# One run of state sums a batch, a scan over the states, and blocks laid out by GpSimd in a linear-attention layer

## The reference

```
xn  = layernorm(x)
q, k, v = split(xn @ wqkv);  q = relu(q); k = relu(k)        # 16 heads of 16 channels
num = q_t . sum_{s<=t} k_s v_s^T;  den = q_t . sum_{s<=t} k_s + 1e-5
attn = (num / den) @ wo
cw  = top-2 router weights of sigmoid(xn @ Wr), normalised   # 8 experts
routed = sum_{e<4} cw_e * (silu(xn Wg_e) * (xn Wu_e)) Wd_e
         + (cw_4 + cw_6) * xn + cw_7 * relu(xn)
conv = causal depthwise convolution of xn, 4 taps, + conv_b
out = x + attn + routed + conv
```

## Time and profile before

| | us |
|---|---|
| median of 3 runs | 1347.9 (1345.97 to 1350.45) |
| the profiled execution, its own time | 1346.54 |
| its span, first to last instruction | 1344.8 |
| PE busy | 1313.8 (98%) |
| DVE busy | 1114.9 (83%) |
| POOL busy | 814.9 (61%) |
| ACT busy | 738.3 (55%) |

### The profile page before, as it was taken

How to read it: one execution, slowest core, us unless ns; L and a number is a source line. 1 busy time by engine, 2 the same in 40 slices (tenths; PEclk the granted TensorE clock), 3 DMA queues, 4 the chain that set the end, 5 groups by cost and what they waited for, 6 DMA issues and landing times.

```text
span 1344.8 us, 54748 instructions
## 1 busy us (share of the span) xinstructions
PE 1313.8 (98%) x24384; PEld 1136.4 (85%) x24384; DVE 1114.9 (83%) x2566; ACT 738.3 (55%) x1545; POOL 814.9 (61%) x679
## 2 busy tenths in 40 slices
PE   4899999999999999999999999999999999999997
PEld 3788888888888888888888888888888888888886
DVE  4888888888888888988888988888888889888885
ACT  4555665555664565654555655555645656545561
POOL 2755666755666656657556666556566566575554
PEclk9999999999999999999999999999999999999999
DMA  4011111111111211111111111121111111111110
GB/s 148 34 66 65 51 48 34 65 65 66 46 53 34 65 65 64 35 45 55 66 65 51 48 35 65 65 65 42 56 35 66 65 65 35 34 65 50 50 49 18
DMA packets 46779, 73.73 MB, mean 55 GB/s; under 512 B 6480, under 2 KB 42192, under 8 KB 42448
## 3 DMA queue, kind: packets, MB, share of 16 engines
q1 hardware_dynamic: 46544, 70.24, 15.1%
HBM read 53.18 MB, written 17.04 MB: 52 GB/s over the span
## 4 chain that ended last, share of the span: by engine, by line
PE 97%; DVE 1%; SPq 1%; ACT 1%; DMA 1%; issue 0%; DVEq 0%
PE ring L300 51%; PE scores L300 17%; PE ring L408 7%; PE ring L422 6%; PE scores L357 5%; PE state_sum L371 4%; PE ring L440 2%; PE scores L310 2%; PE scores L339 2%; DMA x_t<-in_L_attn_x_dram 1%; SPq L257 0%; DVE cT L775 0%; ACT qp L517 0%; DVE sm L753 0%; ACT xn L528 0%
## 5 line engine op out<-in xcount | busy, mean ns | idle before, releaser
L626 POOL TENSOR_TENSOR hid<-hid,cwb 128x512 f32<-128x512 f32 x128 | 169.8, 1327 | 202.6 <-DVE hid L783 200.8
L775 DVE SCALAR_TENSOR_TENSOR cT<-xT,conv_ws,cT 128x512 f32<-128x512 f32 x192 | 288.8, 1543 | 0.0
L614 POOL TENSOR_TENSOR x_t<-x_t,same 128x1024 f32<-128x1024 f32 x32 | 77.1, 2409 | 264.3 <-ACT same L524 264.3
L540 ACT ACTIVATE sg<-ring 128x512 f32<-128x512 f32 x128 | 76.7, 599 | 281.5 <-PE ring L300 281.5
L300 PE MATMUL ring<-xl,wgu_h 128*128 128x512 f32 x512 | 212.0, 414 | 0.0
L300 PE MATMUL ring<-xh,wgu_l 128*128 128x512 f32 x512 | 202.5, 396 | 0.0
L300 PE MATMUL ring<-xh,wgu_h 128*128 128x512 f32 x512 | 201.8, 394 | 0.0
L630 POOL TENSOR_TENSOR hl<-hid,hh 128x512 fp32r<-128x512 f32 x128 | 193.2, 1509 | 0.0
L783 DVE TENSOR_TENSOR hid<-ring,sg 128x512 f32<-128x512 f32 x128 | 88.2, 689 | 110.9 <-PE ring L300 110.9
L480 ACT ACTIVATE yh<-yT 128x256 fp32r<-128x256 f32 x128 | 53.5, 418 | 228.9 <-DVE yT L796 228.9
L753 DVE TENSOR_TENSOR sm<-scores,causal_s 128x512 f32<-128x512 f32 x256 | 158.7, 681 | 20.4 <-PE scores L357 20.2
(11 more groups left out here) (110 smaller groups left out, 3542.6 us busy)
## 6 DMA issues: line engine op xcount, KB each, us to landing
cwb<-cw_rows SPq DMA_DIRECT2D x32, 1024.0 KB, 4.6
x_t<-in_L_attn_x_dram SPq DMA_DIRECT2D x32, 512.0 KB, 4.4
out_dram<-x_t SPq DMA_DIRECT2D x32, 512.0 KB, 2.9
cw_rows<-cwt SPq DMA_DIRECT2D x128, 2.0 KB, 1.4
sm<-in_L_attn_wqkv_dram SPq DMA_DIRECT2D x2, 384.0 KB, 5.5
sm<-in_L_ffn_Wg_dram SPq DMA_DIRECT2D x2, 256.0 KB, 4.2
sm<-in_L_ffn_Wu_dram SPq DMA_DIRECT2D x2, 256.0 KB, 5.8
cwb<-in_L_ffn_Wd_dram SPq DMA_DIRECT2D x1, 512.0 KB, 4.2
```

The lines of the kernel that those rows point to most:

```text
L614: pool.tensor_tensor(xb, xb, same[:, :, :], ALU.add).then_inc(s_base1, 1)
L626: pool.tensor_tensor(hid[:, e, :], hid[:, e, :], cwb[:, e, :], ALU.mult).then_inc(s_hid, 1)
L775: ins = dve.scalar_tensor_tensor(out=cT[:, c, :], in0=xT[:, j % 2, c, n:n + BT], scalar=conv_ws[:, c, n:n + 1], in1=cT[:, c, :], op0=ALU.m ...
```

## The change

The bank of `state_sum` is gone, and with it the running sum on PE. `state_sums` forms the sums of all eight chunks of a batch in one run, after `output(0)` (chunk halves h in the score banks 2 and 3, each chunk in its own columns). ACT copies them to `sums`, laid out with nine places for each state element: place 0 is the state carried in, 1 to 8 the chunks. DVE adds them up in one `tensor_tensor_scan` over 64 x 9 elements, where `keep` is 0 at place 0 and 1 elsewhere; the result, `states`, lies in the memory of `qks_tok`. Place 8 is copied to place 0 of `sums` for the next batch (at a sequence's end a zero is written). POOL multiplies `states` with the mask of equal heads into `state_bd`, which now has a slot for each chunk, in two instructions of 1024 elements a partition; it reads `states` with the chunk as the outer index, so that neighbouring elements of the read lie nine floats apart. The scores of the next batch wait for ACT's copies, as they use the same banks.

The freed bank makes the ring four banks wide. Gates go two tiles ahead of the numerators, which are made for two tiles at once (`numerators(0)`, `numerators(1)`), and DVE, ACT and POOL get lists in that order. The cross products wait once a group for all blocks (`s_bd`).

```diff
-state_bd = sb("state_bd", [P, 4, D])
+sums = sb("sums", [P, C * BLK, NCH + 1])
+state_bd = sb("state_bd", [P, NCH, D])
+keep = sb("keep", [P, C * BLK, NCH + 1])
...
+states = qks_tok[:, :, :].rearrange("p g n -> p (g n)")[:, 0:C * BLK * (NCH + 1)].rearrange(
+    "p (c n) -> p c n", c=C * BLK)
...
-SB = [bank(f"scores{f}") for f in range(ROWS)]
-ring = ctx.enter_context(nc.psum_tensor("ring", [P, 3, BT], F32))
-R = [ring[:, 0, :], ring[:, 2, :]]
-MID = ring[:, 1, :]
-ST_ = bank("state_sum")
-ST = ST_[:, 0:C * BLK].rearrange("p (g n) -> p g n", g=C)
-GB = [R[0], R[1]]
-UB = [R[1], R[0]]
-NB2 = [(R[0], MID), (MID, R[1])]
+low = ctx.enter_context(nc.psum_tensor("scores", [P, ROWS, BT], F32))
+SB = [low[:, f, :] for f in range(ROWS)]
+SUMS = low[:, 2:4, 0:T * C * BLK].rearrange("p h (t c) -> p h t c", t=T)
+ring = ctx.enter_context(nc.psum_tensor("ring", [P, 4, BT], F32))
+B = [ring[:, b, :] for b in range(4)]
+GB = [B[0], B[1], B[2], B[1]]
+UB = [B[2], B[3], B[3], B[0]]
+NUM = [ring[:, 0:2, :], ring[:, 1:3, :]]
...
-VB = [SB[2], SB[3], R[0], R[1]]
-OB = [MID, R[0], R[1], MID]
+VB = [SB[2], SB[3], B[3], B[0]]
+OB = [B[0], B[2], B[1], B[3]]
...
         if u:
             pe.wait_ge(s_sm, at(s, j, U * ROWS, ROWS))
         else:
-            pe.wait_ge(s_qp2, at(s, j, C, k * C + C))
             pe.wait_ge(s_ktok, at(s, j, C, k * C + C))
+            pe.wait_ge(s_sums, at(s, j, 2, 2 * k + 2))
...
-    def state_sum(s, j, k, n):
...
+    def state_sums(s, j, k):
+        pe.wait_ge(s_qp2, at(s, j, C, k * C + C))
+        pe.wait_ge(s_ktok, at(s, j, C, k * C + C))
+        for t in range(T):
+            for g in range(C):
+                for m in range(PPG):
+                    rows = slice(BLK * m, BLK * m + BLK)
+                    for h in range(2):
+                        toks = slice(h * HALF, (h + 1) * HALF)
+                        ins = mm(SUMS[rows, h, t, g * BLK:(g + 1) * BLK], ktok[toks, t, g, rows],
+                                 vp[toks, t, g * PPG + m, 0:3:2, :], start=t == 0 and g == 0, stop=True,
+                                 skip_group_check=True)
         ins.then_inc(s_st, 1)
...
+                if t < 2:
+                    pe.wait_ge(s_out, at(s, j, T, 2 * t + u + 1))
+                elif t == 2:
+                    pe.wait_ge(s_gu, at(s, j, T, 1 + u))
...
+                    pe.wait_ge(s_y, at(s, j, T, 2))
+                product((GB, UB)[u][t], [(wgu_h[:, u, t, c, :], wgu_l[:, u, t, c, :], xh[:, p, c, :],
+                                         xl[:, p, c, :]) for c in range(C)]
...
-        def numerators(t):
...
-                state_sum(s, j, 0, 2 * t + 1)
...
-                n = 2 * t + h
-                pe.wait_ge(s_bd, chunk_at(s, j, n))
+        def numerators(v):
+            pe.wait_ge(s_sg, at(s, j, T, 2 * v + 2))
+            pe.wait_ge(s_sm, at(s, j, U * ROWS, ROWS * (v + 1)))
+            for tt in range(2):
+                t = 2 * v + tt
...
+                    gs = slice((tt * C + g) * HALF, (tt * C + g + 1) * HALF)
+                    for par in range(2):
+                        for m in range(PPG):
+                            pair = g * PPG + m
+                            for h in range(2):
+                                toks = slice(h * HALF, (h + 1) * HALF)
+                                window = vp[toks, t, pair, par:par + 2, :].rearrange("p a d -> p (a d)")
+                                mm(NUM[v][BLK * m:BLK * m + BLK, h, gs], window,
+                                   sm[toks, v, tt, 2 * pair + par, :], start=tt == 0 and par == 0 and g == 0,
+                                   stop=False, skip_group_check=True)
+            pe.wait_ge(s_bd, at(s, j, 1, 1))
+            for tt in range(2):
+                for h in range(2):
+                    n = 2 * (2 * v + tt) + h
+                    if j == 0 and n == 0:
+                        continue
+                    for g in range(C):
+                        gs = slice((tt * C + g) * HALF, (tt * C + g + 1) * HALF)
+                        for w in range(2):
+                            rows = slice(w * HALF, (w + 1) * HALF)
+                            cols = slice(g * P + w * HALF, g * P + (w + 1) * HALF)
+                            ins = mm(NUM[v][rows, h, gs], state_bd[:, n, cols],
+                                     qT[:, g, n * HALF:(n + 1) * HALF], start=False, stop=True,
+                                     skip_group_check=True)
             ins.then_inc(s_num, 1)
-            if t < T - 1:
-                state_sum(s, j, 0, 2 * t + 2)
...
-                scores(s, j, 0, 1)
-            if t == 1 and not last:
-                for c in range(C):
-                    turn_xn(s, j, 1, c)
+        gate_up(0)
+        scores(s, j, 0, 1)
+        gate_up(1)
+        numerators(0)
+        if not last:
+            for c in range(C):
+                turn_xn(s, j, 1, c)
+        gate_up(2)
+        gate_up(3)
+        numerators(1)
         if not last:
             heads(s, j, 1)
         for t in range(T):
-            if t == T - 1 and not last:
+            output(t)
+            if t == 0 and not last:
+                state_sums(s, j, 1)
+            if t == 2 and not last:
                 scores(s, j, 1, 0)
-                state_sum(s, j, 1, 0)
-            output(t)
...
         ins.then_inc(s_relu7, 1)
+        act.wait_ge(s_st, at(s, j, 1, k + 1))
+        for h in range(2):
+            copy(sums[:, :, 1 + h:NCH + 1:2].rearrange("p c t -> p t c"), SUMS[:, h, :, :]).then_inc(s_sums, 1)
         act.wait_ge(s_den, at(s, j, 1, k + 1))
         act.activation(dene[:, :, :], den[:, :, :], ACT.Copy, bias=EPS_DEN).then_inc(s_dene, 1)
...
         silu(0)
         first_tap()
-        high_y(0)
         silu(1)
         high_hid(0)
+        high_y(0)
         high_y(1)
         if not last:
             fill_xT(s, j, 1)
+        high_hid(1)
         silu(2)
         if not last:
             high_x(s, j, 1)
-        high_hid(1)
-        high_y(2)
         silu(3)
         high_hid(2)
+        high_hid(3)
+        high_y(2)
         high_y(3)
-        high_hid(3)
         if not last:
             heads(s, j, 1)
...
+    def blocks(s, j, k):
+        pool.wait_ge(s_scan, at(s, j, 1, k + 1))
+        for g in range(C):
+            ins = pool.tensor_tensor(state_bd[:, :, g * P:(g + 1) * P].rearrange("p n (m c) -> p n m c", m=PPG),
+                                     states[:, g * BLK:(g + 1) * BLK, 0:NCH].rearrange("p c n -> p n c")
+                                     .unsqueeze(2).to_broadcast([P, NCH, PPG, BLK]),
+                                     same_head_s[:, :].rearrange("p (m c) -> p m c", m=PPG).unsqueeze(1)
+                                     .to_broadcast([P, NCH, PPG, BLK]), ALU.mult)
+        ins.then_inc(s_bd, 1)
...
         if not last:
             normalise(s, j, 1)
         weigh(0)
-        low_y(0)
         weigh(1)
         low_hid(0)
+        low_y(0)
         low_y(1)
+        low_hid(1)
         if not last:
             for c in range(C):
                 low_x(s, j, 1, c)
         weigh(2)
-        low_hid(1)
+        low_hid(2)
+        weigh(3)
+        low_hid(3)
         low_y(2)
-        weigh(3)
-        low_hid(2)
         low_y(3)
-        low_hid(3)
         if not last:
             base(s, j, 1)
+            blocks(s, j, 1)
...
-    def blocks(s, j, k, n):
-        dve.wait_ge(s_st, chunk_at(s, j + k, n))
...
+    def sum_states(s, j, k):
+        flat = lambda v: v.rearrange("p c n -> p (c n)")
+        dve.wait_ge(s_sums, at(s, j, 2, 2 * k + 2))
+        dve.tensor_tensor_scan(flat(states), flat(keep[:, :, :]), flat(sums[:, :, :]), 0.0, ALU.mult,
+                               ALU.add).then_inc(s_scan, 1)
+        dve.wait_ge(s_scan, at(s, j, 1, k + 1))
+        if (j + k + 1) % BPS:
+            dve.tensor_scalar(sums[:, :, 0], states[:, :, NCH], 1.0, None, ALU.mult)
+        else:
+            dve.memset(sums[:, :, 0], 0.0)
...
-            if t < T - 1:
-                blocks(s, j, 0, 2 * t + 2)
-            elif j < BPS - 1:
-                blocks(s, j, 1, 0)
-            dve.wait_ge(s_num, at(s, j, T, t + 1))
+            dve.wait_ge(s_num, at(s, j, U, t // 2 + 1))
...
-            if t < T - 1:
-                blocks(s, j, 0, 2 * t + 3)
-        for t in range(T):
-            gate_up(t)
-            attend(t)
-            if t == 0:
-                mask(s, j, 0, 1)
-            else:
-                tap(t)
+        gate_up(0)
+        mask(s, j, 0, 1)
+        gate_up(1)
+        attend(0)
+        attend(1)
+        tap(1)
+        gate_up(2)
+        tap(2)
+        gate_up(3)
+        tap(3)
+        attend(2)
+        attend(3)
...
         for t in range(T):
             if t == 2 and not last:
                 inverses(s, j, 1)
+                sum_states(s, j, 1)
             if t == 3 and not last:
                 mask(s, j, 1, 0)
-                blocks(s, j, 1, 1)
             dve.wait_ge(s_base2, at(s, j, 1, 1))
```

(40 more changed lines are left out.)

46 lines of the change are left out of this document (3 added, 43 removed).

## The result

The changed kernel takes 1405.0 us (1400.2 to 1409.2) beside 1346.9 us of the kernel before: a ratio of 1.043, interval 1.038 to 1.047, 58 us slower. The forecast was 1382, 34 slower, in a range of 1333 to 1410.

A forecast was written before the change was run, and what follows sets the result against it. It took TensorE (98% busy, 40.94 us a batch) as the bound, then a new POOL loop of 42.0: 31 x (42.0 - 40.94) = +33, ends +1, on 1346.5 gives 1380.5, forecast 1382 us; range 1333 to 1410.

The forecast's parts named there:

- PE's own work: PE's instructions in a batch: 7.2 us go out, 6.9 come in, leaving 40.7 us a batch (40.2 to 41.2).
- X: Time of POOL's two 1024-element block instructions: 6.1 us taken, 4.1 if the stepped read costs nothing, 9.6 if doubled.
- the 0.64: Cost in ns an element of a second input on POOL, taken as the stepped read's price: 0.66 us for 1024.
- From there each us of X is one us a batch: Above X = 5.3 the loop through POOL, 35.9 + X, exceeds the ktok loop and sets the batch time.
- this rival: Stepped read free, PE waits for ktok before the state sums: 41.2 us a batch, 1357 (1348 to 1365); chance 0.14.
- H: Moment ACT starts the heads copies (vp): forecast T+23.0, later than before by 0.5 us.
- The loop of 42.0: Loop from H through states, POOL's blocks and weigh(1) to the next H: 16.3 + 6.1 + 4.6 + 15.0 us.
- 35.9: The loop through POOL without X, in us: 16.3 + 4.6 + 15.0.
- four cost 1.9: POOL's way from weigh(1) to H: of six tap halves, four collide with POOL, about 0.47 us each.
- T: Start of gate_up(0) in a batch; H was put at T+23.0, or 22.0 after T without any collision.
- Where PE waits: PE waits for ACT's score before the q projection and ktok before the state sums, about 1 us a batch together.
- The ends: Start of the run +3 us (first scores wait for ACT), end -2 (no last taps before output); taken as +1.

The follow-up runs named there:

- experiment 8: Changed kernel with the blocks' step on the write and ACT's heads copies ahead of high_hid(3), high_y(2), high_y(3); two runs: 1337.9 and 1342.2 us.
- experiment 2: Changed kernel with DVE first copying the states into chunk order, so POOL's blocks read and write neighbours; 1367.6 us, ratio 1.016.
- experiment 3: Changed kernel with a third block instruction on POOL ahead of the two, written to free memory; 1498.5 us, ratio 1.113.
- experiment 1: Changed kernel with POOL's blocks reading neighbours and writing with the step; 1359.6 us, ratio 1.010.
- experiment 7: Changed kernel with ACT's vp and score copies ahead of high_hid(3), high_y(2) and high_y(3), blocks unchanged; 1364.8 us, ratio 1.013.
- experiment 6: Changed kernel with POOL's two low_x moved from in front of weigh(2) to behind it; 1403.1 us, ratio 1.042.
- Experiment 10: The kernel of experiment 8 with two value products of the heads between the second numerators' masked and cross products; 1350.6 us, ratio 1.002.

## Why the prediction was right, and where its size was off

- **PE's own work** was mis-sized by a little. From the rows above the numerators take 477.48 - 476.07 = 1.41 (forecast 1.6), the cross products 1.08 (1.1), the run of sums 1.2 to 1.28 (1.5). PE alone needs 40.0 a batch, as experiment 8 shows, not 40.7. It mattered little, since PE didn't set the pace.
- **X** was right: 5.9 for a forecast of 6.1. That a stepped read costs more was right too: neighbours cost 2.40 (experiment 2), the stepped read 0.59 more, 0.58 ns an element. That this is so near the 0.64 (0.66 in all) taken for it is luck: that row prices one more input, and no run shows that the two are one cost.
- The rule of the Trainium skill (GPSIMD Engine Reference, Performance pitfalls for Q7 kernels) pointed the right way: an estimate from its figure puts the read at 0.85 more and X at 6.5; the measured penalty is 0.7 of that.
- **"From there each us of X is one us a batch"** was right above 5.3 (experiment 3: 3.0 for 3.03). Below it X no longer sets the pace: with X = 4.1 (experiment 1) the batch takes 41.36 for 41.2 reckoned. The number agrees, the wait doesn't: PE waits for `score`, not for `ktok`, so this rival's size was met partly by luck. Moving three ACT copies out of H's way brings that kernel to 40.0 in the first half of its run (experiment 8 against 1), so what follows H was the next bound; with the full X the same move shortens the way to H, and with it the POOL loop (experiment 7).
- **The loop of 42.0** is the term that was mis-sized: the mean period is 43.0. The long and the short batch exaggerate it, as they are cut at PE's `gate_up(0)`; cut at H, loops of 43.1 and 42.4 follow each other. The pieces of the second, by the lines below: from H (494.39) to the states (509.56 + 1.49 = 511.05) 16.7, reckoned 16.3; X 5.9 for 6.1; from there to `weigh(1)`, which starts at 520.27 + 1.26 = 521.53, 4.5 for 4.6; to the next H (536.83) 15.3 for 15.0. Over the 30 hand-overs from the second on, the timelines give 16.5, 5.9, 4.5 and 15.8 on average, with 0.1 in front of the blocks: 42.8.

H (ACT's first `vp` copy) in the two batches, and between them the scan, the blocks and the first two `weigh`:

```profile
494.39 0.37 ACT L488 ACTIVATE vp<-scores 128x256 f32<-128x256 f32 x1
...
509.56 1.49 DVE L788 TENSOR_TENSOR_SCAN qks_tok<-keep,sums 128x576 f32<-128x576 f32 x1
...
511.14 5.92 POOL L637 TENSOR_TENSOR state_bd<-qks_tok,tables_s 128x1024 f32<-128x1024 f32 x2 [1.29 <-DVE qks_tok L788]
...
520.27 2.52 POOL L651 TENSOR_TENSOR hid<-hid,cwb 128x512 f32<-128x512 f32 x2
...
536.83 0.36 ACT L488 ACTIVATE vp<-scores 128x256 f32<-128x256 f32 x1
```

- **The step that failed** is thus the way from `weigh(1)` to H, "four cost 1.9", 0.47 a collision: 15.8 where 15.0 was reckoned, by turns about 15.1 and 16.5. The forecast let every collision cost POOL a little. In the long batch it is DVE that is held, tap 1 alone by 5.9 us (7.37 for two halves of 0.74), and POOL then stands 1.89 us waiting for DVE's `hid`, a wait that the sum left out: from 476.61 + 1.26 = 477.87 to 494.39 it takes 16.5. Experiment 2 shows the loop without it: X is 4.8 and the copy with its wait 0.7, the reckoned loop 35.9 + 5.5 = 41.4, and from the third on the batches take 41.4 on average (42.9 in the changed kernel, where 35.9 + 5.9 = 41.8). (A slip besides: without any collision the recorded terms give H = 7.95 + 11.9 + 1.2 = T+21.05, not 22.0; the forecast doesn't rest on it.)
- **Where PE waits** was half wrong. The forecast named ACT's `score`, about 1 us a batch together with `ktok`. Measured are 7.9 us for `score` in all and 40.1 us for `sg`, in 14 long waits, a wait that the forecast left out. After them the granted clock is lower (0.96 and 0.93 in the windows), and PE is busy 1 to 2.5 us longer in those batches; no term of the sum had it. In the long batch that is not on the way to H: PE's cross products end at 491.66, and DVE takes them up only at 493.29, behind its last tap.
- **The ends** cancel, as said (+3 and -2): the first `gate_up(0)` starts at 39.54, 2.9 later than before (36.68), and what follows the last one is 3.2 shorter (34.96 of 38.13).

The profiled executions lie 1409.2 - 1346.5 = 63 apart, where the sum had 34: the missing 29 are 31 x (43.0 - 42.0) = 31, less 1 for the ends and 1 because the mean batch before took 40.97, not 40.94. Between the medians 24 are missing. Most of this goes with the held tap, as experiment 2 shows; how much of it is the hold itself and how much the waits and the lower clock behind it is not settled, as no run takes away one of them alone.

## What to carry to other kernels

When a step is moved to an engine that is idle 39% of the time, sum up the loop that it closes, not the engine's busy time: here POOL was free, but its two instructions stood between one batch's states and the next batch's gates. In such a loop the layout of one instruction (2.10 against 2.99 us) and the order of three copies on another engine decide between 4% slower and 0.5% faster, and each of the two alone still loses. A hold on one engine is worth removing only if what removes it doesn't stand in the same loop elsewhere.

## What the runs showed of the hardware that was not expected

- POOL's two-input product of 1024 float32: stepped read (36 bytes) 2.99 us, neighbours 2.40, neighbours read with a stepped write and the mask read with a repeated element 2.10. The slower layout isn't the one with the stepped write.
- A DVE instruction with two SBUF inputs was held off for as long as POOL worked without a gap: a pair of tap halves took 7.37 us beside POOL's unbroken row, which went on for 485.50 - 479.35 = 6.15 us after the tap began; with the row 2.5 us shorter (experiment 6) it took 4.87, and in the next batch of the changed kernel 2.05. The hold is not shared evenly: of POOL's instructions beside it the two `low_x` are the longest drawn out, 1.27 for the 1.09 of the fastest.
- In all kernels with the change PE pauses in the second half of the run, 14 to 19 us in all with one pause in batch 2; from batch 20 on nearly every batch has one, in most kernels in the cross products; the kernel before shows none. Experiment 10 moved them and did not lessen them by much. What the traces do show beside them is the queue that the page calls `instruction`, in front of the pause of experiment 8 at 1110.87, for example (window 1108 to 1112):

```profile
q8 instruction: 1, 0.02, 1.4%
```

That transfer starts at 1108.50, 2.4 us before PE goes on. In the 13 profiles of kernels with the change all 215 pauses end 2.2 to 3.0 us after such a transfer starts, also where experiment 10 moved them. So PE probably waits there for its own instructions. That isn't shown: no run changes this queue, most of the 192 transfers of a run have no pause behind them, and the kernel before has 191 and no pause. What experiment 8 would gain without the pauses (18.0 us in all) was not run.
